# The last attention steps and the hand-over to the gathered FFN: a head of o_proj, a block of scalings and a semaphore clear change places

## The chip, the cores and the metric

One core of a Trainium2 chip runs the whole program. The metric is the device time of one execution in microseconds, the median of several runs. TensorE is called PE, VectorE DVE, ScalarE ACT, GpSimd POOL and SyncE SP, as in the profile. All engines run their own instruction streams in order; they meet at semaphores (`wait_ge` and `then_inc`).

## The reference, cut to what matters

Two layers of a gated cross-attention block on x, 8 blocks of 128 tokens by 512. What the change touches is the end of the first attention and what follows it:

```python
x = x + tanh(g_xattn[0]) * L0_xattn(layernorm(x), ctx, mask, wq, wk, wv, wo)  # 32 heads, 8 kv heads
x = x + tanh(g_ffn[0]) * L0_ffn(layernorm(x), up, down, perm)
    # t = x[:, perm]; gelu(t_h @ up_h) @ down_h per head h of 32 columns; t[:, argsort(perm)]
x = x + tanh(g_xattn[1]) * L1_xattn(layernorm(x), ctx, ctx, Wt, Wp, Wg, Wz, gn_w, gn_b)
    # t = Wt@v, p = Wp@q, g = Wg@k; att = sum(p*g) per group; y = Wz@(att*t); group norm; + ctx
x = x + tanh(g_ffn[1]) * L1_ffn(layernorm(x), gate, experts)   # one of 8 experts a token
```

## The kernel before

**Stages.** `project_kv` makes keys and values, `attention` the first attention, `middle` the permuted FFN and the second attention, `experts` the routed FFN. Products that must be accurate are three matmuls: each operand is split into a high part (float32r, a copy by ACT) and a low part (a subtraction by DVE or POOL), and hi·hi, hi·lo and lo·hi are added in PSUM.

**Attention.** A unit u = 8g + b is key-value head g (four query heads) on block b. Each engine has a list of stages with an offset, (stage, ahead), and a step s calls stage(s + ahead) in the list's order (`run`, L497 to L522); this list is the only order there is, and each engine has its own. On PE a step is scores(s), the sums of squares and the query projection of later units, p_transpose(s-1), o_proj(s-2), values(s-1). The softmax of a unit goes DVE mask and maximum (L779, L784), ACT exps (L592), DVE reciprocal (L812), POOL normalisation (L695), PE transposes (L903), ACT and DVE split pT (L610, L816), PE values (L927 to L929), ACT and DVE split oT (L587, L768), PE o_proj (L916 to L918, twelve matmuls, three a head), DVE accumulation into x (L822) and LayerNorm statistics (L88, only for g = 7).

For 8g + b from UNITS - QAHEAD = 58 on, the second list of each engine, the last stages, is used: no query projection is left (steps 58 to 65, the drain). In it sit pieces of the next stage as well: `z01`, `z2`, `z3` (products of the context with a combined matrix, into banks that have come free), and in step 63 `transpose_x`, which turns the first four blocks of the normalised x after POOL (L730) and DVE (L851) have made them. On PE its place is between o_proj(61) and values(62). DVE's list in the drain is oT_split(-2), mask_max(0), normalise_ln2(-4), pT_split(-1), the query sums, p_recip(0), accumulate(-2), copy_xT(-4), x_stats(-2). ACT's is oT_split(-2), pT_split(-1), v_split, exps(0), copy_z01, copy_xT(-4), copy_z23. `oT_hi` and `oT_lo` are single buffers; ACT's oT_split(u) waits until o_proj(u-1) is done.

**Middle.** PE does z_product(4) to (7) (L1310), the last two behind the last accumulation. ACT takes Ln and Exp of the variance (L1076, L1078), DVE a Newton step (L77 to L83) and the shift (L112), DVE and ACT normalise blocks 4 to 7 (L1212, L1081), PE transposes them (L1346), DVE and ACT copy them out (L1217, L1086). SP stores the transposed x in halves, `xT_scr[0]` and `[1]` (L1056); POOL gathers its rows in permuted order by four indirect DMAs a half (L1184). Twelve packs follow, four of 512 tokens from the first half and eight of 256 from the second: PE up (L1363), ACT Gelu (L1120), PE down (L1373), DVE copy to yT (L1243). POOL scatters each copied pack row by row to `yT_scr` (L1157), in three parts of 4, 2 and 2 blocks, each four indirect DMAs; SP loads each part back (yU, L1060) when its four have landed. PE transposes it (L1320), DVE adds it to x and takes statistics (L1249, L103), `g_product` (L1314) and `p_product` (L1329) lead to the second attention.

**POOL's queue there.** Gather 0; `scale_ctx` of blocks 0 and 1 (L1151, after col_step); gather 1; `scale_ctx` 2 and 3; scatter(0, jt), each followed by one scaling; `clear_and_free_semaphores` and the `recycled` flag (L1192); scatter(1, ·); scatter(2, ·); then `add_ctx` and `rstd3`. ACT loads its Gelu table (L1114) behind its last copy of the transposed x. PE waits for all copies of xT and z (L1350 to L1352) ahead of pack 0.

Of the kernel before, what the change touches and what calls it, by code (L numbers as in the profile page):

```python
# [28 lines left out]
P = 128  # L29
B = 8  # L30
# [396 lines left out]
def attention(nc, d, s, block):  # L427


    with ExitStack() as ctx:  # L430
# [18 lines left out]
        oT_hi = m.sb("oT_hi", [P, D], F32R)  # L449
        oT_lo = m.sb("oT_lo", [P, D], F32R)  # L450
# [37 lines left out]
        xT_ps, z_ps = [s.ps[i] for i in (0, 1, 4, 5)], [s.ps[i] for i in (0, 3, 0, 1)]  # L488
# [92 lines left out]
        def _(act):  # L581
            act.wait_ge(qeps_set, 1)

            def oT_split(u, b, g, odd):
                act.wait_ge(pv_done, u + 1)
                reached(act, o_done, u)
                act.activation(oT_hi[:, :], oT_ps[:, :], ACT.Copy).then_inc(oT_hi_done, 1)  # L587
# [163 lines left out]
        def _(dve):  # L751
# [14 lines left out]
            def oT_split(u, b, g, odd):  # L766
                dve.wait_ge(oT_hi_done, u + 1)
                dve.tensor_tensor(oT_lo[:, :], oT_ps[:, :], oT_hi[:, :].bitcast(F32), ALU.subtract)\  # L768
# [91 lines left out]
        def _(pe):  # L860
# [46 lines left out]
            def o_proj(u, b, g, odd):  # L907
# [4 lines left out]
                for h in range(HG):  # L912
                    if b == 0:
                        pe.wait_ge(wo_lo_done, 4 * g + h + 1)
                    oh, ol = oT_hi[:, h * P:(h + 1) * P], oT_lo[:, h * P:(h + 1) * P]
                    pe.matmul(o_ps[b % 2][:, :], oh, wo_hi[odd][:, h, :], start=(h == 0), stop=False)  # L916
                    pe.matmul(o_ps[b % 2][:, :], ol, wo_hi[odd][:, h, :], start=False, stop=False)  # L917
                    last = pe.matmul(o_ps[b % 2][:, :], oh, wo_lo[odd][:, h, :], start=False, stop=(h == HG - 1))  # L918
                last.then_inc(o_done, 1)
# [42 lines left out]
            def z3(u, b, g, odd):  # L962
                if after(u, b, g, B - 1):
                    pe.wait_ge(xT_copied[1], 2)
                    z_product(3)

            pe.wait_ge(s.mid_ld, 16 * 10)
            pe.matmul(oT_ps[:, 0:P], s.wt[:, :], s.wzT[:, :], start=True, stop=True).then_inc(mT_done, 1)
            run(pe, [(scores, 0), (sum_squares, 4), (q_proj, 6), (p_transpose, -1), (o_proj, -2), (values, -1)],
                [(scores, 0), (sum_squares, 4), (z01, 0), (p_transpose, -1), (z2, -1), (o_proj, -2),  # L970
                 (transpose_x, -4), (values, -1), (z3, -1)])


def middle(nc, d, s, block):


    with ExitStack() as ctx:
# [91 lines left out]
        def _(act):  # L1069
# [38 lines left out]
            copy_z(5)  # L1108
            act.wait_ge(xshift_done, 1)
# [4 lines left out]
            act.preload_act_table(ACT.Gelu)  # L1114
# [33 lines left out]
        def _(pool):  # L1148
# [28 lines left out]
            for c in range(2):  # L1177
                if c:
                    pool.wait_ge(ctx_nat_ld, 16)
                    pool.wait_ge(col_step, 2)  # L1180
                    scale_ctx(range(2))
# [5 lines left out]
            scale_ctx(range(2, 4))  # L1187
            for jt in range(KT):
                scatter(0, jt)
                scale_ctx(range(4 + jt, 5 + jt))  # L1190
            nc.clear_and_free_semaphores(s.stage_sems)
            pool.memset(s.recycled_flag[:, :], 0.0).then_inc(s.recycled, 1)  # L1192
            for jt in range(KT):
                scatter(1, jt)
# [807 lines left out]
```

## Time and profile before

| | us |
|---|---|
| three runs | 792.78, 793.20, 797.03 |
| median | 793.2 |
| the profiled execution, in all | 797.66 |
| its span | 795.9 |
| busy: PE, DVE, ACT, POOL | 755.1, 459.6, 430.5, 274.5 |
| mean granted TensorE clock | 0.982 |

The span is what the trace shows of one execution; 1.8 us lie around it. The trace's times start at zero with the span. A row of the chain of waits is a piece of the path that ended last. In a timeline a row is an instruction or a merged run of equal ones, with the idle time before it and what ended that in brackets. "L916" is a line of the kernel. A granted clock of 1.00 is 2.4 GHz, 0.50 is 1.2 GHz.

### The profile page before, as it was taken

To read this page: it belongs to the slowest core of one execution; us is meant where nothing else is said; L and a number is where in the kernel's file an instruction comes from. 1 tells how busy PE (TensorE), PEld (TensorE's weight loads), DVE (VectorE), ACT (ScalarE), POOL (GpSimd) and SP (SyncE) were. 2 spreads that over 40 slices of the span, in tenths; PEclk is the share of its full clock that TensorE was granted. 3 is DMA by queue.
4 is the path that set the end of the run, shared out by engine and by line. 5 is a ranking of instruction groups with operands and counts; after the bars stand their busy time and mean duration, and the time that the engine had idled before them with its cause. 6 is when DMAs were issued, how large, how long until landed. Compare 5 with 4: busy or idle time off the path is not lost.

```text
span 795.9 us, 12734 instructions
## 1 busy us (share of the span) xinstructions
PE 755.1 (95%) x3975; PEld 592.2 (74%) x3975; DVE 459.6 (58%) x1038; ACT 430.5 (54%) x1274; POOL 274.5 (34%) x431
## 2 busy tenths in 40 slices
PE   5999989899999999999999999999999987987997
PEld 3888877788888888888888888888887743555775
DVE  4786411556465656564655565656558764787652
ACT  4543315556556556555655655655555466557831
POOL 0331005234334233424423523433322438624242
PEclk9999999999999999999999999999999999797999
DMA  8545461132041140140131203203142135664232
GB/s 303 180 133 172 133 189 46 49 150 76 15 173 37 57 173 28 54 183 15 66 119 80 66 30 158 80 15 120 34 131 85 54 109 184 240 261 158 73 109 76
DMA packets 42126, 87.82 MB, mean 110 GB/s; under 512 B 5561, under 2 KB 26041, under 8 KB 38226
## 3 DMA queue, kind: packets, MB, share of 16 engines
q1 hardware_dynamic: 38884, 78.71, 28.7%
q0 software_dynamic: 3184, 8.41, 3.1%
q8 instruction: 27, 0.44, 0.2%
q14 instruction: 31, 0.25, 0.1%
HBM read 70.28 MB, written 35.57 MB: 133 GB/s over the span
## 4 chain that ended last, share of the span: by engine, by line
PE 71%; DVE 6%; ACT 3%; POOL 2%; DMA 2%; issue 1%; POOLq 0%; DVEq 0%; SPq 0%
PE banks L882 8%; PE banks L916 7%; PE banks L884 7%; PE banks L883 7%; PE banks L918 7%; PE banks L917 7%; PE banks L868 6%; PE banks L903 3%; PE banks L895 2%; PE banks L1831 2%; PE banks L1830 2%; PE banks L1832 2%; PE banks L927 2%; PE banks L929 2%; PE banks L928 2%
## 5 line engine op out<-in xcount | busy, mean ns | idle before, releaser
L592 ACT ACTIVATE p_sb<-p_sb,nmax 128x128 f32<-128x128 f32 x256 | 99.7, 391 | 62.7 <-DVE nmax L784 62.5
L587 ACT ACTIVATE oT_hi<-banks 128x512 fp32r<-128x512 f32 x64 | 38.2, 597 | 140.1 <-PE banks L929 140.1
L822 DVE SCALAR_TENSOR_TENSOR x_sb<-banks,tgates,x_sb 128x512 f32<-128x512 f32 x64 | 48.0, 749 | 70.8 <-PE banks L918 70.8
L690 POOL TENSOR_TENSOR v_lo<-v_raw,v_hi 128x128 fp32r<-128x128 f32 x64 | 29.5, 461 | 133.6 <-ACT v_hi L635 133.6
L779 DVE SCALAR_TENSOR_TENSOR p_sb<-banks,q_rstd,mask 128x128 f32<-128x128 f32 x256 | 71.5, 342 | 4.5 <-POOL q_rstd L83 4.0
L868 PEld LDWEIGHTS banks<-kT,qT_sb 128*128 128x128 f32 x512 | 67.7, 193 | 5.9 <-issue 0.5
L695 POOL TENSOR_TENSOR p_sb<-p_sb,rsum 128x512 f32<-128x512 f32 x64 | 66.5, 1040 | 15.2 <-DVE rsum L812 15.2
L868 PE MATMUL banks<-kT,qT_sb 128*128 128x128 f32 x512 | 68.2, 277 | 0.1
L768 DVE TENSOR_TENSOR oT_lo<-banks,oT_hi 128x512 fp32r<-128x512 f32 x64 | 44.1, 689 | 33.0 <-ACT oT_hi L587 33.0
L400 PE MATMUL banks<-w_hi,ctx_hi 128*128 128x512 f32 x128 | 54.1, 422 | 9.0 <-DVE ctx_lo L331 9.0
L816 DVE TENSOR_TENSOR pT_lo<-banks,pT_hi 128x512 fp32r<-128x512 f32 x64 | 44.2, 690 | 24.9 <-ACT pT_hi L610 24.9
L916 PE MATMUL banks<-odd_hi,oT_hi 128*128 128x512 f32 x128 | 53.6, 419 | 2.4 <-DVE oT_lo L768 2.2
L812 DVE RECIPROCAL rsum<-prob_sum 128x4 f32<-128x4 f32 x64 | 11.3, 177 | 73.8 <-ACT p_sb L592 73.7
L882 PE MATMUL banks<-xT_hi,w_hi 128*128 128x512 f32 x128 | 53.7, 420 | 0.0
L882 PE MATMUL banks<-xT_hi,odd_hi 128*128 128x512 f32 x128 | 53.7, 419 | 0.0
L916 PE MATMUL banks<-w_hi,oT_hi 128*128 128x512 f32 x128 | 53.6, 419 | 0.0
L402 PE MATMUL banks<-w_lo,ctx_hi 128*128 128x512 f32 x128 | 51.2, 400 | 0.0
L401 PE MATMUL banks<-w_hi,ctx_lo 128*128 128x512 f32 x128 | 51.1, 400 | 0.0
L884 PE MATMUL banks<-xT_hi,w_lo 128*128 128x512 f32 x128 | 50.8, 397 | 0.0
L918 PE MATMUL banks<-w_lo,oT_hi 128*128 128x512 f32 x128 | 50.6, 396 | 0.0
L918 PE MATMUL banks<-odd_lo,oT_hi 128*128 128x512 f32 x128 | 50.6, 395 | 0.0
L917 PE MATMUL banks<-w_hi,oT_lo 128*128 128x512 f32 x128 | 50.6, 395 | 0.0
(276 smaller groups left out, 1901.9 us busy)
## 6 DMA issues: line engine op xcount, KB each, us to landing
sorted_x<-in_empty SPq DMA_DIRECT2D x8, 2064.0 KB, 9.7
w_raw<-in_wq_l SPq DMA_DIRECT2D x8, 1024.0 KB, 5.1
w_raw<-in_wo_l SPq DMA_DIRECT2D x8, 1024.0 KB, 4.8
exp_w<-in_exp_w_l SPq DMA_DIRECT2D x8, 1024.0 KB, 9.3
kT_scr<-kT_st SPq DMA_DIRECT2D x16, 256.0 KB, 2.3
v_scr<-v_st SPq DMA_DIRECT2D x16, 256.0 KB, 2.3
xs<-sorted_x SPq DMA_DIRECT2D x15, 258.0 KB, 2.8
v_raw<-v_scr SPq DMA_DIRECT2D x14, 256.0 KB, 2.6
```

The lines of the kernel that those rows point to most:

```text
L400: pe.matmul(kv_ps[i % 3][:, :], ctx_hi[:, kt, tok], hi, start=(kt == 0), stop=False)
L402: last = pe.matmul(kv_ps[i % 3][:, :], ctx_hi[:, kt, tok], lo, start=False, stop=(kt == KT - 1))
L592: last = act.activation(p_sb[:, b % 2, h * P:(h + 1) * P], p_sb[:, b % 2, h * P:(h + 1) * P], ACT.Exp, bias=nmax[:, b % 2, h:h + 1], accum ...
L695: pool.tensor_tensor(blocks(p_sb[:, b % 2, :]), blocks(p_sb[:, b % 2, :]), per_block(rsum[:, b % 2, :], P), ALU.mult).then_inc(p_done, 1)
L779: last = dve.scalar_tensor_tensor(out=p_sb[:, b % 2, cols], in0=s_ps[:, cols], scalar=rstd[:, c, h * HB + bb:h * HB + bb + 1], in1=mask[:, :],
L868: last = pe.matmul(s_ps[:, h * P:(h + 1) * P], qT_sb[:, c, h, bb * P:(bb + 1) * P], kT[:, b * P:(b + 1) * P], start=True, stop=True)
L882: pe.matmul(q_ps[b % 2][:, :], hi, xh, start=(kt == 0), stop=False)
L883: pe.matmul(q_ps[b % 2][:, :], hi, xl, start=False, stop=False)
L884: last = pe.matmul(q_ps[b % 2][:, :], lo, xh, start=False, stop=(kt == KT - 1))
L916: pe.matmul(o_ps[b % 2][:, :], oh, wo_hi[odd][:, h, :], start=(h == 0), stop=False)
L917: pe.matmul(o_ps[b % 2][:, :], ol, wo_hi[odd][:, h, :], start=False, stop=False)
L918: last = pe.matmul(o_ps[b % 2][:, :], oh, wo_lo[odd][:, h, :], start=False, stop=(h == HG - 1))
```

## The change

1. oT gets two buffers, and ACT's oT_split(u) waits for o_proj(u-2) only.
2. In the drain o_proj is cut in two: `o_first` does heads 0 to 2 (nine matmuls), then values(s-1), then `o_last` head 3 (three) and o_done. `transpose_x` comes behind o_last.
3. z_product(4) moves from `middle` into step 65, ahead of o_first(63).
4. ACT loads the Gelu table between the Exp of the variance and the normalising.
5. POOL scales all eight context blocks ahead of gather 1, once the shift of LayerNorm is there, and none later.
6. The semaphore clear stands behind all twelve scatters.
7. PE's waits ahead of pack 0 are spread over packs 0 and 1.

```diff
-        oT_hi = m.sb("oT_hi", [P, D], F32R)
-        oT_lo = m.sb("oT_lo", [P, D], F32R)
+        oT_hi = m.sb("oT_hi", [P, 2, D], F32R)
+        oT_lo = m.sb("oT_lo", [P, 2, D], F32R)
...
-                reached(act, o_done, u)
-                act.activation(oT_hi[:, :], oT_ps[:, :], ACT.Copy).then_inc(oT_hi_done, 1)
+                reached(act, o_done, u - 1)
+                act.activation(oT_hi[:, b % 2, :], oT_ps[:, :], ACT.Copy).then_inc(oT_hi_done, 1)
...
+            def o_first(u, b, g, odd):
                 pe.wait_ge(oT_lo_done, u + 1)
                 reached(pe, acc_done, u - 1)
                 if after(u, b, g, B - 3):
                     pe.wait_ge(s.z_copied[1], 2)
+                o_heads(u, b, g, odd, range(HG - 1))
+
+            def o_last(u, b, g, odd):
+                o_heads(u, b, g, odd, (HG - 1,)).then_inc(o_done, 1)
...
+            def z4(u, b, g, odd):
+                if after(u, b, g, B - 1):
+                    pe.wait_ge(pT_lo_done, UNITS)
+                    z_product(4)
...
-                [(scores, 0), (sum_squares, 4), (z01, 0), (p_transpose, -1), (z2, -1), (o_proj, -2),
-                 (transpose_x, -4), (values, -1), (z3, -1)])
+                [(scores, 0), (sum_squares, 4), (z01, 0), (p_transpose, -1), (z2, -1), (z4, -2), (o_first, -2),
+                 (values, -1), (o_last, -2), (transpose_x, -4), (z3, -1)])
...
             copy_z(5)
+            act.wait_ge(xseed_done, 2)
+            act.preload_act_table(ACT.Gelu)
             act.wait_ge(xshift_done, 1)
             normalise2(5)
             normalise2(7)
             copy_xT(5)
             copy_xT(7)
-            act.preload_act_table(ACT.Gelu)
...
                     pool.wait_ge(ctx_nat_ld, 16)
+                    pool.wait_ge(xshift_done, 1)
                     pool.wait_ge(col_step, 2)
-                    scale_ctx(range(2))
+                    scale_ctx(range(B))
...
-            scale_ctx(range(2, 4))
-            for jt in range(KT):
-                scatter(0, jt)
-                scale_ctx(range(4 + jt, 5 + jt))
+            for c in range(3):
+                for jt in range(KT):
+                    scatter(c, jt)
             nc.clear_and_free_semaphores(s.stage_sems)
             pool.memset(s.recycled_flag[:, :], 0.0).then_inc(s.recycled, 1)
-            for jt in range(KT):
-                scatter(1, jt)
-            for jt in range(KT):
-                scatter(2, jt)
...
-            pe.wait_ge(s.pT_lo_done, UNITS)
-            z_product(4)
...
-            pe.wait_ge(xT_copied[0], 3)
-            pe.wait_ge(xT_copied[1], 5)
-            pe.wait_ge(z_copied[1], HB + 2)
...
-                            if k == 0 and i == 2:
-                                pe.wait_ge(z_copied[0], 2)
+                            if k == 0:
+                                pe.wait_ge(z_copied[i // 2 == 0], HB + 2 if i == 0 else 2)
+                            if k == 1 and i == 0:
+                                pe.wait_ge(xT_copied[0], 3)
+                                pe.wait_ge(xT_copied[1], 5)
```

## Rows read from the trace of the kernel before

**Rows 1.** The page, part 2: granted clock, 40 slices of 19.9 us.

```profile
PEclk9999999999999999999999999999999999797999
```

**Rows 2.** Chain of waits, one period: start us, us, what.

```profile
607.36 1.14 DVE p_sb L779 x4
...
608.52 0.70 DVE nmax L784
...
609.25 1.66 ACT p_sb L592 x7
...
610.93 0.04 DVE rsum L812
...
611.02 0.75 DVE x_sb L822
...
611.79 0.70 DVE bn L88
...
612.62 0.66 DVE oT_lo L768
```

**Rows 3.** Timeline of PE: start us, us, engine line op, out<-in, count.

```profile
607.31 0.50 PE L916 MATMUL banks<-odd_hi,oT_hi 128*128 128x512 f32 x1 [0.40 <-DVE oT_lo L768]
...
609.98 0.39 PE L918 MATMUL banks<-odd_lo,oT_hi 128*128 128x512 f32 x1
...
610.67 0.40 PE L929 MATMUL banks<-pT_lo,v_hi 128*128 128x512 f32 x1
...
629.64 1.53 PE L941 MATMUL banks<-ident_sb,hid 128*128 128x128 f32 x12 [0.83 <-POOL hid L730]
```

**Rows 4.** Timeline of DVE, end of the drain.

```profile
628.47 0.68 DVE L816 TENSOR_TENSOR pT_lo<-banks,pT_hi 128x512 fp32r<-128x512 f32 x1
...
641.91 0.75 DVE L822 SCALAR_TENSOR_TENSOR x_sb<-banks,tgates,x_sb 128x512 f32<-128x512 f32 x1 [3.15 <-PE banks L918]
```

**Rows 5.** Timelines of DVE and ACT; last, line L851 alone, ns min/median/max.

```profile
644.32 0.58 DVE L77 TENSOR_TENSOR xtmp<-xseed 128x4 f32<-128x4 f32 x1 [0.38 <-ACT xseed L1078]
644.93 0.21 DVE L79 TENSOR_TENSOR xtmp<-xtmp,xval 128x4 f32<-128x4 f32 x1
...
649.18 1.28 ACT L1114 ACT_TABLE_LOAD   x1
650.47 1.94 ACT L1120 ACTIVATE hid<-banks 128x1024 f32<-128x1024 f32 x2
...
L851 DVE TENSOR_SCALAR hid<-x_sb,mv,xrstd x2: 704/845/986, 626.9 to 627.6; 128x512 f32<-128x512 f32 x2
```

**Rows 6.** Timeline of POOL.

```profile
644.12 1.52 POOL L1151 TENSOR_SCALAR ctx_res<-ctx_nat,tgates,tb 128x512 f32<-128x512 f32 x2 [3.44 <-DVE tb L1226]
...
661.27 1.02 POOL L1157 DMA_INDIRECT yT_scr<-xg,perm_col  x1 [0.17 <-issue]
...
679.28 0.97 POOL L1157 DMA_INDIRECT yT_scr<-xg,perm_col  x1 [0.30 <-issue]
```

**Rows 7.** Chain of waits, from the second store to the transposes.

```profile
649.21 5.34 DMA xT_scr<-xT
...
667.29 2.79 DMA yT_scr<-xg,perm_col
...
670.09 5.64 DMA xT<-yT_scr
...
675.87 3.64 PE banks L1320 x16
```

**Rows 8.** One-us window: length, PE, PEld, DVE, ACT, POOL busy (count), clock, DMA.

```profile
680.00:681.00 1.00, 1.00 (x6) 1.00 (x6) 1.00 (x3) 0.00 (x0) 0.98 (x2) 0.50 1.11 422
```

**Rows 9.** Timelines of DVE and PE, the first stage behind the load.

```profile
676.99 1.60 DVE L1249 SCALAR_TENSOR_TENSOR x_sb<-banks,tgates,x_sb 128x512 f32<-128x512 f32 x2 [5.91 <-PE banks L1320]
...
687.43 1.41 DVE L1249 SCALAR_TENSOR_TENSOR x_sb<-banks,tgates,x_sb 128x512 f32<-128x512 f32 x2 [3.67 <-PE banks L1320]
...
681.30 5.65 PE L1314 MATMUL banks<-ctx_nat,wgT 128*128 128x512 f32 x8
```

More of the change, by code:

```diff
@@ L487, in attention @@
         s.q_done, s.o_done, s.acc_done, s.pT_lo_done, s.oT_lo_done = q_done, o_done, acc_done, pT_lo_done, oT_lo_done
-        xT_ps, z_ps = [s.ps[i] for i in (0, 1, 4, 5)], [s.ps[i] for i in (0, 3, 0, 1)]
+        xT_ps, z_ps = [s.ps[i] for i in (0, 1, 4, 5)], [s.ps[i] for i in (0, 3, 0, 1, 6)]
         def after(u, b, g, last):
@@ L767, in oT_split @@
                 dve.wait_ge(oT_hi_done, u + 1)
-                dve.tensor_tensor(oT_lo[:, :], oT_ps[:, :], oT_hi[:, :].bitcast(F32), ALU.subtract)\
+                dve.tensor_tensor(oT_lo[:, b % 2, :], oT_ps[:, :], oT_hi[:, b % 2, :].bitcast(F32), ALU.subtract)\
                     .then_inc(oT_lo_done, 1)
@@ L905, in p_transpose, with o_heads @@
                 last.then_inc(pT_done, 1)
-            def o_proj(u, b, g, odd):
+            def o_heads(u, b, g, odd, heads):
+                for h in heads:
+                    if b == 0:
+                        pe.wait_ge(wo_lo_done, 4 * g + h + 1)
+                    cols = slice(h * P, (h + 1) * P)
+                    oh, ol = oT_hi[:, b % 2, cols], oT_lo[:, b % 2, cols]
+                    pe.matmul(o_ps[b % 2][:, :], oh, wo_hi[odd][:, h, :], start=(h == 0), stop=False)
+                    pe.matmul(o_ps[b % 2][:, :], ol, wo_hi[odd][:, h, :], start=False, stop=False)
+                    last = pe.matmul(o_ps[b % 2][:, :], oh, wo_lo[odd][:, h, :], start=False, stop=(h == HG - 1))
+                return last
+            def o_first(u, b, g, odd):
                 pe.wait_ge(oT_lo_done, u + 1)
@@ L911, in o_proj @@
                     pe.wait_ge(s.z_copied[1], 2)
[L912 to L919, printed above, removed]
+                o_heads(u, b, g, odd, range(HG - 1))
+            def o_last(u, b, g, odd):
+                o_heads(u, b, g, odd, (HG - 1,)).then_inc(o_done, 1)
+            def o_proj(u, b, g, odd):
+                pe.wait_ge(oT_lo_done, u + 1)
+                reached(pe, acc_done, u - 1)
+                o_heads(u, b, g, odd, range(HG)).then_inc(o_done, 1)
             def values(u, b, g, odd):
```

## The prediction, made before the changed kernel ran

> **What bounds the kernel now.** I read the clock row of the page first [rows 1]: TensorE is at full clock except late, in the slice from 676.5 us (and the one from 716 us). The steady attention steps are TensorE's own, back to back, and the change adds and removes nothing there (a second oT buffer, no matmul more). So only what follows step 58 counts, and I went through the chain of waits from there. Call a unit u = 8g+b; in step s PE does scores(s), p_transpose(s-1), o_proj(s-2), values(s-1). The drain is steps 58 to 65.
>
> In the drain TensorE no longer sets the pace. One period of the chain [rows 2] is mask 607.36, nmax 608.52, exps 609.25, reciprocal 610.93, accumulate 611.02, bn 611.79, oT_lo 612.62, next mask 613.28: 1.16 + 0.73 + 1.68 + 0.09 + 0.77 + 0.83 + 0.66 = 5.92 us, a ring of VectorE and ScalarE. The accumulate starts 0.09 behind the reciprocal. Its other condition, o_done, was met earlier: the last o_proj matmul starts 609.98 and lasts 0.39, so 610.40 [rows 3].
>
> After the drain the chain is: last accumulate, LayerNorm, transposes, store, gather, twelve packs, GpSimd's scatters, load of yU, transposes of y, updates, and on into the experts, which nothing here touches.
>
> **Drain: last head behind the values.** Twelve matmuls of o_proj take 2.67 from first start to last, three more put the last value matmul at 610.67 [rows 3]: 0.23 each, 0.34 for the first behind a wait. Now values comes three matmuls (0.70) sooner and o_done 0.70 later. Who wants either? The ScalarE copy oT_hi(s-1) gets its input sooner, but VectorE does accumulate(s-2) and bn(s-2) ahead of oT_lo(s-1), in this order, unchanged. So an early pv_done buys nothing, and a late o_done delays the whole VectorE queue: oT_lo, the next mask, the next scores.
>
> Worse, values waits for pT_lo, which VectorE writes right behind nmax, and o_last now stands behind that wait. The new ring: mask to nmax 1.16; pT_lo 0.60 behind it, 0.68 long (line L816 [rows 4]), 0.04 for the release: 1.32; six matmuls 0.34 + 5 x 0.23 less the last's start, that is 1.26 to the last start, then 0.40 and 0.03: 1.69; accumulate 0.77; bn to oT_lo 0.83; oT_lo to mask 0.66. Sum 6.43 against 5.92: +0.51 a step, in steps 58 to 61: +2.0. Step 62, where two z products stand in front of the transpose, adds 0.25: oT_lo(61) is 2.25 late.
>
> Step 63: VectorE's pT_lo(62), at 628.47 [rows 4], stands behind two LayerNorm operations, so it comes at 630.7 and ends 631.4. PE idles before values(62), then six matmuls: o_done(61) at 631.4 + 1.7 = 633.1. transpose_x stood ahead of the values, where it filled a gap; it now stands behind o_last: 12 transposes took 1.53 from 629.64, to 631.2 [rows 3]; 16 take 2.0, to 635.1. VectorE's copy of the fourth block waits for that, 3.9 longer. ScalarE's three copies hold oT_hi(62) back too, by less. With bn(61) behind that copy, oT_lo(62) is 3.8 late. Step 64: o_done(62) a further 0.70 behind the values, accumulate(62) about 4.5 late. In step 65 no values follow, so no more is lost. z4 moves into the gap before o_first(63), which is idle time: nothing on the path; its old place after the last accumulate was covered as well, by the Newton chain. **Accumulate(63) comes at 641.91 [rows 4] + 4.5 = 646.4.** Bounds: 0 (if the order did not bind) to 5.5 (each step losing another 0.15 to releases). I take 4.5 because each link has a row.
>
> **LayerNorm to second gather.** Two scalings ran on GpSimd beside the Newton chain; the first Newton step took 0.58 there, the second, as long a tile, 0.21 [rows 5]; the third was slow again. Now the scalings wait for xshift: the chain wins about 0.6. But all eight then start beside VectorE's and ScalarE's normalising; the same VectorE operation took 0.70 to 0.99 a piece beside GpSimd's in step 63 [rows 5], and I charge 0.3 on the path. Gelu's table load, 1.28 [rows 5], now lies between the seed and xshift on ScalarE: 644.8 to 646.05, where ScalarE was idle; the shift comes 0.6 sooner than before, but ScalarE's half gets none of that. Net -0.2 (-0.6 to +0.3). Eight scalings at 0.76 (two took 1.52, in company that did not slow them [rows 6]) are 6.1, plus 1.4 for company: over by 653 on the old time axis, while the store lands at 654.55 [rows 7]; should they be slower by over 1.6 they delay the gather.
> The relaxed waits let the first Gelu begin about 1.5 sooner, but the first half's packs finished just as the second gather landed, and that one does not move: worth nothing on the path.
>
> A rule against this: the Trainium skill, "ScalarE: Activation LUTs", What ACT_TABLE_LOAD costs, adds a drain of 1.38 us to the 1.28. Here the Gelu starts at 650.47, straight behind the load's end [rows 5], so the trace disagrees; by the rule the result would be 1.3 later.
>
> **Scatters.** Between gather and scatter GpSimd did two scalings, then one behind each scatter: the first scatter at 661.27 [rows 6], the fourth at 667.29 [rows 7]. Now, on the old axis less 0.2: last gather 658.40, scatters every 1.27 (the pitch of the last eight) from 659.67; the fourth at 663.5, the eighth at 668.55, the twelfth at 673.65 against 679.28 [rows 6]. yT is ready in time for each (the fourth copy ends at 660.8, the last at 671.1). The fourth lands 2.8 later and yU[0] takes 5.64 [rows 7]: transposes at 672.15 instead of 675.87, -3.7. Second and third load are there at 677 and 681; the transposes want them at 678.5 and 682.75. Clearing the semaphores costs 0.5 behind the scatters: add_ctx(0,1) at 675.3 to 677.8, its first consumer rstd3 at 679.1. Covered; 1.3 is the slack.
>
> **The clock.** TensorE was idle 3.37 us before 675.87; its granted clock went from 1.00 to 0.50 (2.4 to 1.2 GHz) and stayed there to 685.7 [rows 8]. At the half level sixteen transposes took 3.64 [rows 7], where twelve took 1.53 at the full one [rows 3], and four g products 5.65 [rows 9]. In the changed kernel the g products end at 672.05 and the loads are there at 672.15: no gap, no fall. Then VectorE bounds: update(0) at 672.8 (676.99 before [rows 9]), its group and the group means 6.8 long, update(4) at 679.6 against 687.43 [rows 9]: -7.8, kept to the end since POOL, ScalarE and PE shift as much (-7.8 to -8.2).
>
> **The sum.** On the profiled execution (span 795.9, 797.66 in all): +4.5 - 0.2 - 7.8 = -3.5, so 794.2. But the runs are 792.78, 793.20 and 797.03. With the full clock in 675 to 686, update(4) would have come at 676.45 + 6.8 = 683.3, 4.1 sooner: 797.66 - 4.1 = 793.5, the median. I read the two runs at 793 as runs without the fall, the third and the profile as runs with it. Against those the scatters give only 683.3 - 679.6 = 3.7: 793.2 + 4.5 - 0.2 - 3.7 = 793.8. Both ways say 794; I take 793.9.
> The Trainium skill ("TensorE: Matmul & The Clock Gate", What's actually happening) says the monitor's window runs free of the kernel, so that one gap may or may not bring a fall; one trace cannot show it.
>
> **Rivals.**
> 1. The drain costs nothing: values early lets something start that I overlook. Then 793.2 - 3.9 = 789.3. Against: VectorE's order. 0.13.
> 2. The clock falls in every run of before, and the 4.4 between median and profile is the profiler's. Then 793.2 - 3.5 = 789.7. For: one run only lies at 797. 0.17.
> 3. Slower: the longer idle stretches of the drain (1.7 before values(62), 1 before each of the last two o_projs) drop the clock to 0.50. The one such stretch in the trace cost the 4.1 of above: 798.0. It decides from an idle stretch like that before 675.87 (3.37); the longest I compute is 1.7. 0.10.
> 4. Slower in part: the eight scalings last past 654.5 or yU[1], yU[2] come late, their scatters' packets behind the first load's: +1 to +3, 796. 0.12. With it the table drain by the page's rule, 795.2: 0.04.
>
> **How the numbers follow.** Forecast 0.44, its own range 792 to 796. A measurement of this kernel can tell 0.5%, 4.0 us, from none: faster is below 789.2, slower above 797.2. Faster: half of rivals 1 and 2, 0.15, and 0.02 elsewhere. Slower: rival 3 and a third of 4, 0.14, and 0.03 from a median that falls on runs with a fall. Range 788.9 to 798.2.
>
> **What would show it.** Right: the accumulate to accumulate period in steps 58 to 61 grows from 5.9 to 6.4, last accumulate at 646; PE waits for pT_lo ahead of the values; the distance from last accumulate to the first y update shrinks from 35.1 to about 30.9, and the clock stays at 1.00 between them and update(4). Wrong: a period of 5.9, which leaves only the gain; a table load followed by a pause; a gather released by the last scaling; a clock of 0.50 anywhere before the experts.

## The result, and the profile after

| | before | changed |
|---|---|---|
| median, twelve executions each | 793.62 | 800.03 |
| lowest and highest | 791.36 to 799.30 | 797.62 to 801.59 |
| ratio, with its 95% interval | | 1.0070 (1.0054 to 1.0087) |
| the profiled execution, in all | 797.66 | 800.17 |
| its span | 795.9 | 798.3 |
| mean granted clock | 0.982 | 0.985 |

The changed kernel is 0.7% slower, and 800.03 lies above the range's 798.2. One execution of the kernel before, on occasion F below, took 2603.59 us and is left out of the ratios. The clock row of the page answers to [rows 1]:

```profile
PEclk9999999999999999999999999999999998997999
```

**The drain went as computed.** The accumulates of VectorE, in the timeline (start, length, line, and in brackets the idle time before it and what ended it), answer to [rows 2, 4]:

```profile
606.16 0.75 DVE L822 SCALAR_TENSOR_TENSOR x_sb<-banks,tgates,x_sb 128x512 f32<-128x512 f32 x1 [0.45 <-PE banks L915]
612.53 0.75 DVE L822 SCALAR_TENSOR_TENSOR x_sb<-banks,tgates,x_sb 128x512 f32<-128x512 f32 x1 [0.45 <-PE banks L915]
618.91 0.75 DVE L822 SCALAR_TENSOR_TENSOR x_sb<-banks,tgates,x_sb 128x512 f32<-128x512 f32 x1 [0.46 <-PE banks L915]
...
646.44 0.75 DVE L822 SCALAR_TENSOR_TENSOR x_sb<-banks,tgates,x_sb 128x512 f32<-128x512 f32 x1 [3.15 <-PE banks L915]
```

Before, an accumulate followed the reciprocal by 0.09. Now VectorE waits another 0.45 behind the reciprocal for the last matmul of o_last, and the period is 6.37. The last one comes at 646.44 instead of 641.91. PE's timeline, as in [rows 3], shows why in step 63: the values wait for pT_lo, and o_last stands behind them.

```profile
630.01 0.40 PE L915 MATMUL banks<-odd_lo,oT_hi 128*128 128x512 f32 x1
631.60 0.50 PE L939 MATMUL banks<-pT_hi,v_hi 128*128 128x512 f32 x1 [1.19 <-DVE pT_lo L816]
...
632.87 0.39 PE L915 MATMUL banks<-odd_lo,oT_hi 128*128 128x512 f32 x1
```

**The hand-over came out as a whole.** This is the stretch from the last accumulate to the second gather: VectorE's Newton steps, ScalarE and POOL, against [rows 5, 6]:

```profile
648.85 0.16 DVE L77 TENSOR_TENSOR xtmp<-xseed 128x4 f32<-128x4 f32 x1 [0.38 <-ACT xseed L1095]
...
649.72 1.00 DVE L1226 TENSOR_SCALAR hid<-x_sb,mv,xrstd 128x512 f32<-128x512 f32 x2
...
649.32 1.28 ACT L1127 ACT_TABLE_LOAD   x1
650.61 1.52 ACT L1098 ACTIVATE hid<-x_sb,xshift,xrstd 128x512 f32<-128x512 f32 x2
...
649.97 6.50 POOL L1169 TENSOR_SCALAR ctx_res<-ctx_nat,tgates,tb 128x512 f32<-128x512 f32 x8 [5.34 <-DVE xshift L112]
...
659.34 0.98 POOL L1203 DMA_INDIRECT xg<-xT_scr,perm_col  x1 [2.87 <-DMA xT_scr<-xT]
```

**What nobody had priced is in the packs.** From 664 us on, VectorE (copies to yT) and ScalarE (Gelu) wait for PE, though by their records PE's products are through (a matmul's end in the trace is modelled). First POOL and DVE, then ACT, then PE:

```profile
663.13 0.95 POOL L1203 DMA_INDIRECT xg<-xT_scr,perm_col  x1 [0.30 <-issue]
664.38 1.00 POOL L1175 DMA_INDIRECT yT_scr<-xg,perm_col  x1 [0.30 <-issue]
...
668.26 0.97 POOL L1175 DMA_INDIRECT yT_scr<-xg,perm_col  x1 [0.30 <-issue]
671.60 0.97 POOL L1175 DMA_INDIRECT yT_scr<-xg,perm_col  x1 [2.37 <-DVE xg L1257]
```

```profile
661.80 0.69 DVE L1257 COPY xg<-banks 128x512 f32<-128x512 f32 x1 [0.82 <-PE banks L1385]
...
666.56 0.69 DVE L1257 COPY xg<-banks 128x512 f32<-128x512 f32 x1 [3.26 <-PE banks L1385]
...
670.90 0.42 DVE L1257 COPY xg<-banks 128x256 f32<-128x256 f32 x1 [2.83 <-remote]
```

```profile
668.07 0.60 ACT L1138 ACTIVATE hid<-banks 128x512 f32<-128x512 f32 x1 [3.46 <-PE banks L1375]
```

```profile
663.33 1.06 PE L1385 MATMUL banks<-hid,down 128*32 128x512 f32 x8
664.33 0.71 PE L1375 MATMUL banks<-xg,up 32*128 32x256 f32 x8
664.97 0.64 PE L1385 MATMUL banks<-hid,down 128*32 128x256 f32 x8
...
668.72 1.22 PE L1375 MATMUL banks<-xg,up 32*128 32x256 f32 x4 [2.20 <-ACT hid L1138]
```

The down product of 663.33 should end at 664.39, but its copy starts at 666.56: 2.2 late. The up product of 664.33 ends at 665.04 on paper, its Gelu starts at 668.07: 3.0 late. The down product of 664.97 is copied at 670.90, 5.3 late. The delay sets in as the first scatter goes out. In windows of 2 us (length, busy PE, PEld, DVE, ACT, POOL with counts, clock, DMA share, GB/s):

```profile
664.00:666.00 2.00, 1.79 (x22) 0.65 (x20) 0.00 (x0) 0.60 (x2) 1.39 (x3) 1.00 0.73 231
666.00:668.00 2.00, 0.52 (x4) 0.12 (x3) 1.40 (x3) 0.00 (x0) 1.65 (x2) 0.96 0.68 266
668.00:670.00 2.00, 1.22 (x4) 0.50 (x4) 0.07 (x1) 0.60 (x1) 0.97 (x1) 0.50 0.46 176
670.00:672.00 2.00, 1.22 (x12) 0.41 (x16) 1.06 (x3) 1.55 (x3) 0.40 (x1) 0.50 0.23 86
```

The granted clock is still 1.00 in the first window and falls to 0.50 (1.2 GHz) at 667.8, after the delay has begun, so the fall follows it. The packs end at 681.1 instead of 670.6: 4.5 of that is the drain, 6 the delay with the half clock that it brings (to 674.7). Behind them all goes at the clock of 1.00; update(4), as in [rows 9], comes at

```profile
690.40 1.40 DVE L1263 SCALAR_TENSOR_TENSOR x_sb<-banks,tgates,x_sb 128x512 f32<-128x512 f32 x2
```

### The profile page after: what moved, and what is told of

It reads as the page before. It is cut to its first block, busy times and chain, and to the rows that moved or that the text cites. A ratio compares the mean times of both kernels' runs of the same rounds, so it can differ in the third digit from the quotient of the medians.

```text
span 798.3 us, 12733 instructions
## 1 busy us (share of the span) xinstructions
PE 755.7 (95%) x3975; PEld 589.2 (74%) x3975; DVE 458.8 (57%) x1038; ACT 430.8 (54%) x1274; POOL 275.9 (35%) x431
## 4 chain that ended last, share of the span: by engine, by line
PE 72%; DVE 4%; ACT 3%; POOL 2%; DMA 2%; issue 2%; POOLq 0%; DVEq 0%; ACTq 0%
PE banks L882 8%; PE banks L913 8%; PE banks L915 7%; PE banks L914 7%; PE banks L884 7%; PE banks L883 7%; PE banks L868 7%; PE banks L903 3%; PE banks L895 2%; PE banks L939 2%; PE banks L941 2%; PE banks L940 2%; PE banks L1843 2%; PE banks L1842 2%; PE banks L1844 2%
## 5 line engine op out<-in xcount | busy, mean ns | idle before, releaser
L883 PE MATMUL banks<-xT_lo,w_hi 128*128 128x512 f32 x128 | 50.7, 396 | 0.0
```

The costliest lines, as they stand in the source:

```text
L883: pe.matmul(q_ps[b % 2][:, :], hi, xl, start=False, stop=False)
```

## The experiments

The changed kernel and its parts were measured on seven occasions, each with the kernel before beside it. Medians in us; "late products" says whether the profiles show products of the packs that complete a microsecond or more behind their records.

| occasion | before | the others | late products |
|---|---|---|---|
| A | 793.62 | changed 800.03 | yes |
| B | 793.86 | drain alone 799.86, no drain 789.55, no drain with wait 797.02, no drain with POOL's old spacing 795.39 | none |
| C | 793.95 | changed 793.24, drain and POOL 795.14, drain with table load and waits 800.64, changed with wait 799.21 | none |
| D | 794.60 | changed 793.22, split only 798.32, transposes late only 797.47, POOL only 788.83 | none |
| E | 795.04 | changed 799.46, POOL only 794.22 | in both |
| F | 795.18 | POOL only 788.59, POOL only with wait 794.04 | none |
| G | 795.31 | POOL only 794.34, POOL only with wait 796.82 | in both |

D and G were on the same chip. Each kernel has one profile an occasion, the kernel before one in all, on A.

**1. The drain parts alone** (the first three points of the change on the kernel before).

```diff
-                [(scores, 0), (sum_squares, 4), (z01, 0), (p_transpose, -1), (z2, -1), (o_proj, -2),
-                 (transpose_x, -4), (values, -1), (z3, -1)])
+                [(scores, 0), (sum_squares, 4), (z01, 0), (p_transpose, -1), (z2, -1), (z4, -2), (o_first, -2),
+                 (values, -1), (o_last, -2), (transpose_x, -4), (z3, -1)])
```

> The kernel before with the drain parts of the change alone (two oT buffers, last head behind the values, fourth z product in the drain); POOL's order, the table load, the clear and the waits ahead of the packs stay as before. Theory A (my sums of the drain are right, and what the change lost beyond them it lost in the packs): the last accumulate comes at 646.4 instead of 641.9, the packs keep the length of before (first up product to last down product), and the whole is +4.5 us, about 798. Theory B (the drain also upsets the packs, by another order of banks or a colder clock): the packs' pace falls here too, and the whole is +8 us or more. Theory C (the drain's 4.5 is given back, since the loads of before hid it): under +2 us.

799.86, ratio 1.0073 (1.0048 to 1.0098), that is +5.8 (3.8 to 7.8), for 4.5 expected. Executions don't all reach the drain at the same time, so I count from one accumulate of the attention (545.78 before, 545.85 after, 544.39 here) to the last: 96.13 before, 100.59 in the changed kernel, 100.53 here. The first up product to the last down product takes 21.3 (652.27 to 673.58), as before (649.26 to 670.59). Theory A.

**2. Everything but the drain parts.**

```diff
-                [... (z4, -2), (o_first, -2), (values, -1), (o_last, -2), (transpose_x, -4), (z3, -1)])
+                [... (o_proj, -2), (transpose_x, -4), (values, -1), (z3, -1)])
```

> The changed kernel with the drain parts undone: table load early, eight scalings ahead of the second gather, scatters back to back, clear behind them, relaxed waits. Theory A (packs stall when scatters follow right behind the gathers): the stall of the changed kernel is here as well, 6 us between the fourth up product and the last down product, and the gain of the scatters is nearly used up: 0 to +2 us against before, 794 to 796, update(4) of x no earlier than about 686. Theory B (the stall comes of the drain's later start): no stall, scatters as in my sum, -3.7 to -3.9 us, 789.7.

789.55, ratio 0.9942 (0.9914 to 0.9971). No delay: theory B on this occasion; runs 5 and 14 take it back. Last accumulate 642.18, fourth scatter 663.95, transposes of y 672.49, update(4) 679.78 at full clock, 37.6 behind the accumulate, which is what my sum had.

**3. The same, the first scatter waiting for all four gathers of the second half.**

```diff
+            for jt in range(KT):
+                pool.wait_ge(gathered[KT + jt], 16)
             for c in range(3):
```

> As the run without the drain parts, but POOL waits for the data of all four gathers of the second half before it issues the first scatter. Theory A1 (the stall comes of scatters and gathers being under way together in one software queue): the stall is gone, the first scatter comes about 2.5 us later than without the wait, and the time is that of the scatters' sum less those 2.5: about -1 us against before. Theory A2 (the stall comes of the scatters' own rate, one each 1.3 us, beside the packs' signals): the stall only moves behind the wait, and the time is that of the run without the wait or up to 1 us more. Theory A3 (it is the late start of the packs or the clock): the time doesn't change against the run without the wait by over 1 us, and the stall lies where it was.

797.02. With no delay to cure, it shows the price: the first scatter comes 3.3 later against the last accumulate (21.2 for 17.9), PE then idles 3.64 ahead of the transposes of y, the clock falls to 0.50, and update(4) comes 42.7 behind the accumulate instead of 37.6. The wait costs 5.1 in the profile and 7.5 in the medians; what makes the other 2.4 stays open (the profiled execution was the fastest of its twelve).

**4. No drain parts, POOL's scalings where they were, the clear behind all scatters.**

```diff
-                    pool.wait_ge(xshift_done, 1)
                     pool.wait_ge(col_step, 2)
-                    scale_ctx(range(B))
+                    scale_ctx(range(2))
...
-            for c in range(3):
+            scale_ctx(range(2, 4))
+            for jt in range(KT):
+                scatter(0, jt)
+                scale_ctx(range(4 + jt, 5 + jt))
+            for c in range(1, 3):
```

> As the run without the drain parts, but POOL's scalings stand where they stood before (two ahead of the second gather, two behind it, one behind each scatter of the first part), so of POOL's changes only the clear behind the scatters is left, with the early table load and the relaxed waits. If the scalings between scatters were what spaced them and so kept the packs' pace (theory A), the packs here run as before, no stall, and the whole is within 1 us of before (the clear saves 0.5 to 1 us ahead of the fifth scatter). If the stall comes of the relaxed waits or of the table load (theory D), it is here too and the whole is +4 us or more.

795.39, ratio 1.001 (0.9985 to 1.0035): nothing gained. Behind the last accumulate the fourth scatter comes 1.2 earlier than before, since the store took 4.1 here and not 5.3, but the chain of waits shows that the load behind it eats that up:

```profile
665.98 2.77 DMA yT_scr<-xg,perm_col
668.75 0.02 issue
668.77 8.09 DMA xT<-yT_scr
676.86 0.14 issue
676.99 3.65 PE banks L1320 x16
```

The load of the first part takes 8.09, not 5.64 as in [rows 7]. Its last packet came 7.8 after the issue. It has scatters of the second part beside it, but so had it before and in runs 2, 5 and 12, where the last packet came 5.1 to 5.5 after the issue. Of all twenty profiles three have it late: this one, run 6 (8.3) and run 16 (8.4); in the others it is 5.1 to 5.8. It comes and goes; its cause stays open. What follows is the idle stretch and the half clock of [rows 7, 8] again.

**5. The changed kernel again.**

> The changed kernel itself, profiled and timed again. In its first profile PE's products of the packs from the fourth on signalled up to 3 us behind their records' ends, from 663.8 to 671 us, and no other kernel so far shows such a delay. Theory H1 (the stall belongs to the kernel): it is in this profile too, update(4) of x near 690.4, and the median is 800. Theory H2 (the stall is an accident of one execution): the packs run here as in the run without the drain parts, 12.9 us from the last accumulate to the second gather and 37.6 from the last accumulate to update(4), and the profiled time is about 794.5, if the start of the attention is where it was; the median of 800 would then have another cause.

793.24 (791.34 to 794.25), ratio 0.9982 (0.9964 to 0.9999). Neither theory quite: no delay, as H2 says, but not by chance within one occasion, since all twelve executions here lie under all twelve of the first. From 153 to 663 us the two traces run 0.3 apart, from 685 us on 5.5 to 6.4. The same rows as above:

```profile
664.15 0.69 DVE L1257 COPY xg<-banks 128x512 f32<-128x512 f32 x1 [1.14 <-PE banks L1385]
665.57 0.39 DVE L1257 COPY xg<-banks 128x256 f32<-128x256 f32 x1
```

```profile
664.84 1.08 ACT L1138 ACTIVATE hid<-banks 128x512 f32<-128x512 f32 x2 [0.56 <-PE banks L1375]
```

```profile
664.00:666.00 2.00, 1.94 (x28) 0.91 (x24) 1.82 (x5) 1.37 (x3) 1.62 (x2) 1.00 0.73 244
666.00:668.00 2.00, 1.97 (x28) 0.66 (x24) 1.88 (x5) 1.46 (x3) 1.39 (x3) 1.00 0.61 236
```

```profile
674.70 1.98 PE L1328 MATMUL banks<-ctx_nat,wgT 128*128 128x512 f32 x4
676.65 2.19 PE L1334 MATMUL banks<-ident_sb,xT 128*128 128x128 f32 x16
```

The copy starts 1.14 behind its product's start (663.01; on occasion A it was 3.2), PE is busy throughout, and the transposes follow the g products without a gap and take 2.19 at a clock of 1.00, where [rows 7] had 3.64. Update(4) comes at 683.96, 37.82 behind the last accumulate (646.14); on A it was 43.96, and 45.52 before.

**6 to 8. The drain with other subsets.** Run 6: without the early table load and the relaxed waits. Run 7: with these, POOL as before. Run 8: the whole change and the wait of run 3.

```diff
-            act.wait_ge(xseed_done, 2)
-            act.preload_act_table(ACT.Gelu)
...
             copy_xT(7)
+            act.preload_act_table(ACT.Gelu)
```

> The drain parts with POOL's parts (scalings ahead, scatters back to back, clear behind), without the early table load and without the relaxed waits. If the stall comes of scatters close behind the gathers at this time of the program (theory H1a): stall and 800. If it comes of the table load or the waits, whose only effect is how early PE, ACT and DVE run in the first packs (theory H1b), or is an accident (H2): no stall, 794 to 795.

> The drain parts with the early table load and the relaxed waits, POOL's order as before. Theory H1a: no stall, about the drain alone, 798 to 800. Theory H1b: the stall lies here, 800 or more and update(4) later than 38 us after POOL's scatters of before would give. The relaxed waits alone are worth nothing on the path by my sum, since the first packs end as the second gather lands.

> The changed kernel with POOL waiting for all four gathers of the second half before the first scatter. In the kernels without the drain parts this wait cost 7.5 us in the median but moved the first scatter by 3 us only. Theory H1a: no stall here, the first scatter 3 us later, the whole 796 to 799. Theory H2: about 4.5 us above the kernel without the drain parts and with the wait, 801.

795.14, 800.64 and 799.21, no late products in any. On this occasion they could not tell H1a from H1b, as the changed kernel itself had none. The wait for the gathers costs 6.0 (7.5 in run 3). The drain with table load and waits has the ratio 1.0067 (1.0046 to 1.0089), the drain alone 1.0073, so with POOL's old order those two are worth nothing. With POOL's new order the early table load costs something. In run 6, without it, ScalarE's normalising and the second gather come

```profile
649.65 1.52 ACT L1098 ACTIVATE hid<-x_sb,xshift,xrstd 128x512 f32<-128x512 f32 x2 [0.53 <-DVE xshift L112]
658.36 0.98 POOL L1202 DMA_INDIRECT xg<-xT_scr,perm_col  x1 [2.10 <-DMA xT_scr<-xT]
```

that is 3.39 and 12.10 behind the last accumulate (646.26). In the changed kernel it is 4.17 and 12.90: the normalising waits for the end of the load (650.60), not for the shift. The packs end 28.6 behind the last accumulate with it (runs 2, 5 and 9) and 27.9 without (runs 6, 12, 15 and 16). The medians don't show this: run 6's 795.14 lies above the changed kernel's 793.24, with overlapping intervals, and its profile has the late load of run 4.

**9. The changed kernel for the third time.**

> The changed kernel for the third time. The first time it took 800.0 us (twelve executions, 797.6 to 801.6) with PE held back in the packs from 663.8 to 671 us; the second time 793.2 (twelve, 791.3 to 794.3) with no such delay, while the kernel before took 793.6 and 793.9 on the two occasions. Theory S (the delay belongs to one chip or one loading of the program): this time it is one or the other, all executions alike, near 793 without the delay or near 800 with it. Theory T (it comes at random, execution by execution): times of both kinds among the executions, 793 and 800 mixed.

793.22 (792.09 to 794.82), ratio 0.9975 (0.9960 to 0.9990), all alike: theory S.

**10 and 11. The two drain edits apart**: the last head behind the values with the transposes of x where they were (and the fourth z product back in `middle`), and the transposes behind the values with o_proj whole. The edit of run 10, against the changed kernel:

```diff
-                (values, -1), (o_last, -2), (transpose_x, -4), (z3, -1)])
+                (transpose_x, -4), (values, -1), (o_last, -2), (z3, -1)])
```

> The kernel before with one drain edit only: the last head of the output projection behind the values (two oT buffers), transposes of the first four blocks where they were, ahead of the values. From the accumulate of the attention that starts near 545.8 to the last one it is 96.13 us in the kernel before and 100.6 with all drain parts. By my terms: four steps of +0.51, step 62 +0.25, then only the last head's 0.70 late in step 63, and little in 64: 99.1, a period of 6.37 in steps 58 to 61, the whole +3 us. Rival: the periods are no longer than before and all of the 4.4 comes of the transposes: 96.1.

> The kernel before with the other drain edit only: the transposes of the first four blocks behind the values, the output projection whole. By my terms the periods of steps 58 to 61 stay 5.9; the fourth copy of the transposed x waits for transposes that start behind the values of step 63 instead of at 629.6, 1.5 to 2 us later: 97.6 to 98.1 from the accumulate near 545.8 to the last, the whole +1.5 to +2. Rival: the transposes hide in PE's gap as well there, 96.1, and the split alone carries all 4.4.

From the accumulate near 545 to the last: 100.64 with the split only, +4.51, and 96.88 with the late transposes only, +0.75; medians 798.32 (ratio 1.0040, 1.0011 to 1.0070) and 797.47 (1.0032, 1.0012 to 1.0052). Both sizes were off, and they don't add: 4.46 together. Run 11's median is 2.5 above before (1.0 to 4.1), more than its profile's 0.75; that profile is of the fastest of its ten executions, and the rest stays open. With the split only, the last accumulates are

```profile
624.23 0.75 DVE L822 SCALAR_TENSOR_TENSOR x_sb<-banks,tgates,x_sb 128x512 f32<-128x512 f32 x1 [0.67 <-PE banks L915]
633.03 0.75 DVE L822 SCALAR_TENSOR_TENSOR x_sb<-banks,tgates,x_sb 128x512 f32<-128x512 f32 x1 [2.88 <-PE banks L915]
639.61 0.75 DVE L822 SCALAR_TENSOR_TENSOR x_sb<-banks,tgates,x_sb 128x512 f32<-128x512 f32 x1 [3.24 <-PE banks L915]
645.03 0.75 DVE L822 SCALAR_TENSOR_TENSOR x_sb<-banks,tgates,x_sb 128x512 f32<-128x512 f32 x1 [3.15 <-PE banks L915]
```

Here the transposes stand between pT_lo and o_last, which costs accumulate(61) 1.25 more than in run 1 (631.78), and gives back 1.14 of it a step later, since VectorE's copies come sooner.

**12. POOL's parts alone.** The kernel before with points 5 and 6 of the change.

```diff
+                    pool.wait_ge(xshift_done, 1)
                     pool.wait_ge(col_step, 2)
-                    scale_ctx(range(2))
+                    scale_ctx(range(B))
...
-            scale_ctx(range(2, 4))
-            for jt in range(KT):
-                scatter(0, jt)
-                scale_ctx(range(4 + jt, 5 + jt))
+            for c in range(3):
+                for jt in range(KT):
+                    scatter(c, jt)
...
-            for jt in range(KT):
-                scatter(1, jt)
-            for jt in range(KT):
-                scatter(2, jt)
```

> The kernel before with POOL's parts of the change only: eight scalings ahead of the second gather, scatters back to back, clear behind them. If all the gain of the kernel without the drain parts (-4.3 us) is POOL's, this takes 789.5 as well, the fourth scatter near 663.0 and the transposes of y near 671.7. Rival: without the relaxed waits and the early table load the scatters of the second part run beside the load of the first and its last packets come late, as in the drain with POOL's parts (8.2 us from issue to last packet against 5.4): the transposes near 674.5, PE idle for 2 to 3 us and in part at half clock, 791 to 793.

788.83, ratio 0.9934 (0.9913 to 0.9956): -5.2. All of the gain is POOL's; the transposes come at 672.30 and update(4) at 679.59, 36.9 behind the accumulate of 642.65, 0.7 sooner than in run 2, which has the early table load. (The store ahead of the gather was 1.2 quicker here, but the packs end no sooner than in run 6, where it wasn't.)

**13 and 14. The changed kernel and POOL's parts alone, on one more occasion.**

> The changed kernel for the fourth time, to see whether the first measurement's delay comes back. Theory S (a property of one chip or one loading of the program, rare): 793.2 again, update(4) 37.7 us behind the last accumulate, and no completion of a product over 0.1 us behind its record's end. If it is as common as one measurement in three, the chance to see it here is a third: all executions near 800 then, update(4) 44 us behind the last accumulate.

> POOL's parts alone (eight scalings ahead of the second gather, scatters back to back, clear behind) for the second time, beside the changed kernel on one chip. If the delay of the first measurement belongs to POOL's order on certain chips, this kernel shows it whenever the changed one does, and then takes 795; if it belongs to the combination with the drain parts, this one stays at 788.8 in any case. Without the delay in either, 788.8 again, 4.4 below the changed kernel.

The delay is back, and in both: 799.46 (798.64 to 801.12) and 794.22 (792.01 to 796.09). It doesn't need the drain parts. Run 13's down product of 662.91 is copied at 665.95, run 14's of 656.60 at 661.33, 1.9 and 3.6 later than 1.13 behind its start. The first scatters go out at 663.92 and 656.33. Against occasion D they lose 6.2 and 5.4 us, the kernel before 0.4.

**15 to 18. POOL's parts alone with and without the wait for the gathers, twice.**

```diff
+            for jt in range(KT):
+                pool.wait_ge(gathered[KT + jt], 16)
             for c in range(3):
```

> POOL's parts alone with one more wait: the first scatter only when all four gathers of the second half have landed. If the chip is one that shows the delay (to be seen in the control beside it): theory G (it needs gathers and scatters under way together) says no completion over 0.1 us late here, and a time like the control's or below it, 792; theory R (the scatters' own rate beside busy packs is enough) says the delay starts with the first scatter, 3.5 us later than in the control. On a chip without the delay: the wait moves the first scatter by 2 to 3.5 us and brings back the idle stretch ahead of the transposes of y, and so in part the fall of the clock: 792 to 796 against 788.8.

> POOL's parts alone for the third time, as the control of the kernel with the wait. The first time 788.8 without the delay (chip-wide before 794.6), the second time 794.2 with it (before 795.0). Near 788.8 and no late completions, or near 794 with a product of the packs that completes 3 to 6 us behind its record, in all executions alike.

> POOL's parts alone with the wait for the four gathers ahead of the first scatter, for the second time. Where the control beside it shows the delay: theory G (gathers and scatters under way together are needed) says no completion over 0.1 us late here; theory R (the scatters' rate beside busy packs is enough) says late completions from the first scatter on. Where the control shows none: 794.0 again, 5 above the control, from the idle stretch ahead of the transposes of y and the clock.

> POOL's parts alone for the fourth time, the control: near 788.7 without the delay (chances two in three, by the chips so far), near 794 with it.

First pair: no late products, 794.04 with the wait and 788.59 without (ratio to before 0.9920, 0.9888 to 0.9951). Second pair: late products in both, 796.82 and 794.34. Of the last, the control:

```profile
656.28 1.07 PE L1369 MATMUL banks<-hid,down 128*32 128x512 f32 x8
...
657.18 1.00 POOL L1157 DMA_INDIRECT yT_scr<-xg,perm_col  x1 [0.30 <-issue]
...
660.63 0.69 DVE L1239 COPY xg<-banks 128x512 f32<-128x512 f32 x1 [3.64 <-remote]
```

And the kernel with the wait, in which every gather has landed when the first scatter starts:

```profile
662.91 1.00 POOL L1157 DMA_INDIRECT yT_scr<-xg,perm_col  x1 [3.64 <-DVE xg L1241]
664.22 0.98 POOL L1157 DMA_INDIRECT yT_scr<-xg,perm_col  x1 [0.30 <-issue]
...
663.93 0.39 DVE L1241 COPY xg<-banks 128x256 f32<-128x256 f32 x1
666.43 0.42 DVE L1241 COPY xg<-banks 128x256 f32<-128x256 f32 x1 [1.29 <-PE banks L1371]
671.46 0.42 DVE L1241 COPY xg<-banks 128x256 f32<-128x256 f32 x1 [4.60 <-remote]
```

The last copy that starts as soon as VectorE is free is that of 663.93. The product of 664.43 should be copied at 665.1 (0.71 behind its start, as in run 12) and is at 666.43; the one of 665.65 is copied at 671.46, 5 us late. A small delay comes earlier, with the gathers: the product of 658.63 is copied at 660.25, 0.5 late. The large one has moved behind the wait: as theory R says, and not G. It needs no gather under way. But the pitch of 1.27 alone isn't the trigger either: in every kernel the second half's gathers go out at that pitch beside the packs, and by VectorE's copies no product is over 0.5 late before the first scatter. The kernel before, with scatters 2.0 apart beside the packs and a scaling between them, has no late copy in its profile on A, and its medians on A, E and G are 794.7 on average, against 794.4 on B, C, D and F.

## Why the prediction was right and wrong

**The drain: right, by a sum whose parts were not.** The period (6.43 computed, 6.37 measured, since from oT_lo to the mask it is 0.57 and not 0.66), the wait for pT_lo, accumulate(61) near 633.1 (633.30) and the last accumulate at 646.4 (646.44) came out. Against before, and counted from the accumulate near 545.8, those of units 57 to 63 are late by 1.1, 1.4, 2.0, 2.7, 4.1, 4.4 and 4.5. In time it is less sure: the drain parts alone cost 5.8 (3.8 to 7.8), and the changed kernel on C and D stands 3.7 above run 2, its twin without them, on another occasion. What failed here is the step on transpose_x: I charged the copy that comes 3.9 later as a cause next to the split. Run 11 shows the move alone to cost 0.75, run 10 that the split alone costs all 4.5; at steps 63 and 64 two causes lie beside each other, and the later one counts. Rival 1 is excluded.

**LayerNorm to gather: right within 0.2.** The gather comes 12.90 behind the last accumulate, as before (12.90), where I had -0.2. The Newton steps lose their 0.58 (0.16 each), so the shift comes 0.8 sooner behind the last accumulate; the eight scalings take 6.50 and slow no one: two normalisings take 1.00, as before. But the early table load eats the 0.8, since ScalarE's half then waits for it, as the prediction says; that this half sets the path, and that the gain was there to be had with the load where it was, run 6 shows (3.39 for 4.17, the gather 12.10 for 12.90). What the load's move was to bring is small: the first Gelu starts 7.70 behind the last accumulate with it and the relaxed waits, 7.79 without (run 6), 8.56 before. The table load of 1.28 is followed by the next activation without a pause, at 650.61. By the Trainium skill, "ScalarE: Activation LUTs", What ACT_TABLE_LOAD costs, there would be a drain; the trace disagrees for this place too.

**Scatters and clock: right in the path, wrong in what goes on beside them.** Where no product is late, the changed kernel's update(4) stands 37.7 to 37.8 behind the last accumulate instead of 45.5: -7.7 for my -7.8, and the clock is 1.00 from the packs to past update(4). (In the kernel before, the low clock ends at 685.3, not at the 685.7 of the prediction; it changes nothing.) POOL's parts alone bring -5.2 (-3.5 to -6.9) and -6.4 (-3.9 to -8.9) against medians, for my -3.9; the surplus, as I read it, is that more than the odd execution of before has a clock fall: of 35 on occasion D, the 14 with a mean clock of at least 0.986 took 793.1 on average, the other 21 took 796.1. That fits the reading of the three runs as two kinds, and puts rival 2 between: the fall would be in many executions of before, not in all. It is not shown, as only one of them has a profile and the mean doesn't say where the clock was low.

**The step that failed** is the sentence that yT is ready in time for each scatter. I took the pitch of 1.27 from the last eight scatters, which in the kernel before run when the packs are over [rows 6], and put it beside the packs, with their lengths from a trace in which a scaling stands between any two scatters. The rows allowed the pitch; they said nothing of what goes with it on PE. In its place the runs showed products of the packs that reach VectorE and ScalarE 2 to 5 us late, and with them the copies to yT and the scatters: the fifth scatter waits 2.37 for its copy and starts at 671.60, 7.22 behind the first, where I had 5.1. I had no rival in which TensorE's products come late; the nearest, the fourth (796), had the load of yU late, which the profiles of runs 4, 6 and 16 show, but it is not what happened. On occasions C and D the kernel took 793.2, for 793.9 predicted, and that is in part luck: by the medians the scatters gave 1.3 to 2.5 more than priced and the drain alone took 1.3 more. On A and E it took 800, and the 6 to 7 us between are the delay.

**What is shown and what stays open.** Shown: the delay lies in the packs; the first product over a microsecond late was due 0.1 to 2.2 us behind the start of the first scatter (five profiles); it needs neither the drain parts nor the table load nor the relaxed waits (runs 14, 18), needs no gather under way (17), and comes on some occasions for every kernel measured there with scatters straight behind each other, even on a chip that had shown none (D and G). On those occasions the kernel before was not slower. Argued only: that the scatters' pitch beside busy packs is the trigger, since no kernel but the one before had spaced scatters on such an occasion, and it differs in more than the pitch. Excluded: slow packets. The packets of POOL's queue in the twelve microseconds from the gathers on took 0.159 us on average on A and 0.160 on C. Open is what differs between occasions, and what holds PE. One trace of it: in all five profiles with late products records of semaphores are missing, 5,683 to 5,775 in all where the fifteen others have 6,075 to 6,090; between 660 and 680 us the changed kernel left 122 on A and 394 on C. So the taking of the records may be part of the delay; that it would be there in an execution without records, no run here shows. The Trainium skill, "NOTIFIC — Programmer's Manual", When the ring fills, says that a full ring of records loses the new ones or, set otherwise, overwrites the oldest or stalls the producer. The missing records agree with the first; that the last played a part no run here shows.

## What to carry to other kernels

A work item between two indirect DMAs may look like idle filling and be what spaces them: after closing the gaps, read whether the consumers of the engine that is busy beside them still start on time. In a ring of two engines, ask which instruction the first waits for before putting other matmuls ahead of it; there an early input was worth nothing and a late signal cost 0.5 a step. A preload that is moved into an idle stretch must end before the stretch would: the table load of 1.28 outlasted it by 0.8, once the shift came sooner. When a change has parts that touch different stages, run each alone and on more than one occasion: here POOL's parts alone take 788.7 or 794.3, and the whole change 793.2 or 799.7, beside 793.6 to 795.3 before, so POOL's parts alone are the version to keep.

## What the hardware showed that I had not expected

- A product of PE can reach its consumer 2 to 5 us behind its record with a granted clock of 1.00; the fall to 0.50 comes later (on A the first product so late was due at 664.5, and the clock fell at 667.8).
- A load from memory of 1 MB has its last packet 5.1 to 5.8 us from issue in seventeen profiles and 7.8 to 8.4 in three (runs 4, 6 and 16), with scatters in flight beside it.
- The store ahead of the second gather varies as well: the gather starts 4.4 to 4.5 us behind the last copy of the transposed x in four profiles (runs 4, 11, 12 and 14) and 5.6 to 5.9 in sixteen.
- The same program can be 5.5 us slower in the median on another occasion on the same chip (POOL's parts alone, 788.83 on D and 794.34 on G). Of the changed kernel all 24 executions of C and D (791.3 to 794.8) lie below all 17 of A and E (797.6 to 801.6).
